# The identity multiplied into an unread PSUM bank while TensorE waits, and a shorter setup, in a four-layer graph kernel

## The reference, cut to what matters

```python
A_norm = A + jnp.eye(n)
deg = jnp.sum(A_norm, axis=0) + jnp.sum(A_norm, axis=1) - jnp.diagonal(A_norm)
dinv = jax.lax.rsqrt(deg)
A_hat = A_norm * dinv[:, None] * dinv[None, :]
agg = jnp.einsum('nm,bmd->bnd', A_hat, features)
h = jax.nn.relu(_batchnorm(agg @ W1.T + b1, g1, be1))   # 256 features, over all 32*256 rows
out = _batchnorm(h @ W2.T + b2, g2, be2)                # 128 features, over all rows
x = _layernorm(x + out)
# layer 1: edge attention over 256 edges; layer 2: three adjacency convolutions; layer 3: dense attention
```

## Time and profile before

| | |
|---|---|
| median of 3 runs | 604.58 us |
| the profiled execution, its time | 603.32 us |
| its span | 601.4 us |
| mean granted clock | 0.95 of full |
| TensorE matmul busy | 539.0 us (90%) |
| VectorE busy | 429.6 us (71%) |
| ScalarE busy | 368.4 us (61%) |
| GpSimd busy | 218.3 us (36%) |

### The profile page before, as it was taken

How to read it: one execution, slowest core, us unless ns; L and a number is a source line. 1 busy time by engine, 2 the same in 40 slices (tenths; PEclk the granted TensorE clock), 3 DMA queues, 4 the chain that set the end, 5 groups by cost and what they waited for, 6 DMA issues and landing times.

```text
span 601.4 us, 11286 instructions
## 1 busy us (share of the span) xinstructions
PE 539.0 (90%) x3508; PEld 474.7 (79%) x3508; DVE 429.6 (71%) x1446; ACT 368.4 (61%) x733; POOL 218.3 (36%) x253
## 2 busy tenths in 40 slices
PE   2999799489999879999999999999999999999461
PEld 2888544368787779998998999999999999889361
DVE  5588668678886166358878688787687685756895
ACT  1567692657755415536587686785785776775460
POOL 6750340366575250503516216226126026021231
PEclk9999899789999769999999999999999999999787
DMA  6232100221200000000000100100100100001002
GB/s 188 76 99 70 37 0 0 70 71 36 70 0 1 1 1 1 1 1 1 1 1 2 36 0 1 35 0 0 35 0 0 36 0 10 25 1 37 1 2 70
DMA packets 28382, 15.25 MB, mean 25 GB/s; under 512 B 2320, under 2 KB 28048, under 8 KB 28352
## 3 DMA queue, kind: packets, MB, share of 16 engines
q1 hardware_dynamic: 27792, 13.65, 7.9%
q0 software_dynamic: 560, 1.25, 0.6%
HBM read 10.69 MB, written 4.19 MB: 25 GB/s over the span
## 4 chain that ended last, share of the span: by engine, by line
PE 78%; DVE 13%; ACT 4%; issue 2%; POOL 2%; DMA 1%; DVEq 0%; SPq 0%; ACTq 0%; POOLq 0%
PE psum L237 14%; PE psum L239 14%; PE psum L238 14%; PE psum L1507 9%; PE psum L1332 5%; PE psum L1374 4%; PE psum L1449 2%; PE psum L1459 2%; PE psum L1381 2%; PE psum L1385 2%; PE psum L1395 2%; PE psum L1535 2%; DVE ln_st L183 2%; PE psum L1553 2%; DVE soft L865 2%
## 5 line engine op out<-in xcount | busy, mean ns | idle before, releaser
L202 POOL TENSOR_TENSOR ln_r<-ln_v,mhalf 128x8 f32<-128x8 f32 x32 | 53.3, 1665 | 233.1 <-DVE ln_v L196 233.1
L1507 PE MATMUL psum<-l2w_s,h 128*128 128x128 f32 x512 | 59.7, 275 | 0.0
L1507 PEld LDWEIGHTS psum<-l2w_s,h 128*128 128x128 f32 x512 | 59.0, 192 | 0.7
L237 PE MATMUL psum<-qt_hi,l2w_s_hi 128*128 128x512 f32 x128 | 52.7, 412 | 0.0
L239 PE MATMUL psum<-qt_hi,l2w_s_lo 128*128 128x512 f32 x128 | 50.5, 395 | 0.0
L238 PE MATMUL psum<-qt_lo,l2w_s_hi 128*128 128x512 f32 x128 | 50.4, 394 | 0.0
L231 ACT ACTIVATE keep_x<-keep_x,ln_b,ln_r (+1 forms) x112 | 46.0, 486 | 2.7 <-POOL ln_b L205 2.7
L1175 ACT ACTIVATE h<-psum 128x512 f32<-128x512 f32 x64 | 37.3, 593 | 15.1 <-PE psum L239 15.1
L183 DVE BATCH_NORM_STATS2 ln_st<-keep_x 128x6 f32<-128x128 f32 (+1 forms) x192 | 39.3, 277 | 2.8 <-ACT keep_x L1102 1.7
L237 PE MATMUL psum<-wgt_hi,h_hi 128*128 128x256 f32 x128 | 37.4, 292 | 0.9 <-DVE h_lo L842 0.9
L865 DVE SCALAR_TENSOR_TENSOR soft<-keep_x,wa 128x128 f32<-128x128 f32 x128 | 38.0, 362 | 0.0
(11 more groups left out here) (225 smaller groups left out, 1766.0 us busy)
## 6 DMA issues: line engine op xcount, KB each, us to landing
xin<-in_x SPq DMA_DIRECT2D x64, 128.0 KB, 2.2
out_x<-ob SPq DMA_DIRECT2D x32, 128.0 KB, 1.8
l2w_raw<-in_l2w POOLq DMA_DIRECT2D x1, 512.0 KB, 6.5
adjs<-in_adj SPq DMA_DIRECT2D x1, 256.0 KB, 2.8
adjs<-in_adj_t SPq DMA_DIRECT2D x1, 256.0 KB, 2.9
l2w_s<-in_l2w POOLq DMA_DIRECT2D x1, 256.0 KB, 6.2
w_raw<-in_w_t SPq DMA_DIRECT2D x1, 128.0 KB, 3.2
w2t<-in_w_t SPq DMA_DIRECT2D x1, 128.0 KB, 3.0
```

Source lines behind the costliest of these rows:

```text
L202: pool.tensor_tensor(ln.r[:].rearrange("p s k -> p (s k)"), ln.v[:].rearrange("p s k -> p (s k)"), mhalf[:], ALU.pow).then_inc(ln.root, 1)
L237: pe.matmul(o, lhs[0], rhs[0], start=start, stop=False)
L1507: i = pe.matmul(bank(s)[:, 0, k * D:(k + 1) * D], h2[:, s, g, j * N + t * P:j * N + (t + 1) * P], l2w3_s[:, g, :], start=(g == 0), stop=(g ...
```

## The change

The kernel after differs in these parts.

- `spin(n, bank)` is new: n float32 matmuls of `ident` with `iota_row` (256 columns) into a bank that nobody reads before it is written anew. It stands at five places on TensorE: 4 at the very start, 4 behind the turned roots, 6 behind pass1's edge work, 3 behind pass2's adjacency columns, 6 ahead of the first gather.
- Degrees: the sums along rows come from the accumulating output of two `scalar_tensor_tensor` a tile on VectorE, so that the degree is a 128 x 2 tile. Its root and reciprocal are taken at that size, and TensorE turns them into PSUM bank 0 by two transposes. ScalarE copies the transposed adjacency into `at1`.
- The split of the first weights on VectorE stands behind x0_low(0).
- `coefficients`: `shift = bias - mean` stands ahead of the wait for the root. In the second norm (`turn == 2`) the root and its reciprocal are one power on GpSimd, and the last pair's copy to `oraw` stands inside `coefficients`.
- pass2's statistics read PSUM and stand ahead of the copy; TensorE waits for relu by halves.
- The activation table is loaded behind relu, ahead of the second norm.

```diff
...
@@ -473,6 +473,9 @@
             link(pool.tensor_scalar(same[:], diff[:], 0.0, None, ALU.is_equal))
             pool.tensor_scalar(reset[:], same[:], 1.0, BIG, ALU.subtract, ALU.mult)
 
+            pool.wait_ge(bn_eps, 1)
+            pool.tensor_tensor(bco[:, 1, 2:3], bagg[:, 2:3, 1], mhalf[:, 0:1], ALU.pow).then_inc(bn_root, 1)
+
             pool.wait_ge(adj_dst_out, 1)
             pool.tensor_tensor(prod[:], adj_dst[:], ssrc[:], ALU.mult).then_inc(picked, 1)
 
@@ -594,36 +597,28 @@
 
             dve.wait_ge(pz, 4)
             dve.wait_ge(s_adj, 32)
-            dve.tensor_tensor(degm[:], adj_sb, adjt_sb, ALU.add)
             for t in range(T):
                 blk = slice(t * P, (t + 1) * P)
-                i = dve.tensor_tensor(prod[:, t, blk], adj_sb[:, t, blk], ident[:], ALU.mult)
+                dve.scalar_tensor_tensor(out=degm[:, t, :], in0=adj_sb[:, t, :], scalar=1.0, in1=adjt_sb[:, t, :],
+                                         op0=ALU.mult, op1=ALU.add, accum_out=degc[:, 0, t:t + 1])
+                i = dve.scalar_tensor_tensor(out=prod[:, t, blk], in0=adj_sb[:, t, blk], scalar=1.0, in1=ident[:],
+                                             op0=ALU.mult, op1=ALU.mult, accum_out=degc[:, 1, t:t + 1])
             link(i)
-            for t in range(T):
-                blk = slice(t * P, (t + 1) * P)
-                i = dve.tensor_tensor(degm[:, t, blk], degm[:, t, blk], prod[:, t, blk], ALU.subtract)
-            link(i)
-            for t in range(T):
-                blk = slice(t * P, (t + 1) * P)
-                i = dve.tensor_tensor(degm[:, t, blk], degm[:, t, blk], ident[:], ALU.add)
-            i.then_inc(deg_ready, 1)
-
-            link(dve.tensor_copy(at1[:], adjt_sb))
+            dve.tensor_tensor(degc[:, 2, :], degc[:, 0, :], degc[:, 1, :], ALU.subtract).then_inc(deg_ready, 1)
+
+            dve.wait_ge(at_ready, 1)
             for t in range(T):
                 blk = slice(t * P, (t + 1) * P)
                 i = dve.tensor_tensor(at1[:, t, blk], at1[:, t, blk], ident[:], ALU.add)
             link(i)
 
-            dve.wait_ge(s_small, 16 * SMALL)
-            link(dve.tensor_copy(w1t[0][:], w1_raw[:]))
-            dve.tensor_tensor(w1t[1][:], w1_raw[:], w1t[0][:], ALU.subtract)
-
             dve.wait_ge(deg_root, 1)
-            dve.reciprocal(dinv_bc[:], root_bc[:])
-            link(dve.reciprocal(dinv[:], root[:]))
+            dve.reciprocal(dinv[:], root[:]).then_inc(dinv_ready, 1)
+
+            dve.wait_ge(dinv_spread, 1)
             for t in range(T):
                 i = dve.scalar_tensor_tensor(out=at1[:, t, :], in0=at1[:, t, :], scalar=dinv[:, t:t + 1],
-                                             in1=dinv_bc[:], op0=ALU.mult, op1=ALU.mult)
+                                             in1=bank(0)[:, 0, 0:N], op0=ALU.mult, op1=ALU.mult)
             link(i)
             link(dve.tensor_copy(a_hat[0][:], at1[:]))
             dve.tensor_tensor(a_hat[1][:], at1[:], a_hat[0][:], ALU.subtract).then_inc(a_hat_ready, 1)
@@ -647,6 +642,10 @@
                     i.then_inc(h_stat, 1)
 
             x0_low(0)
+
+            dve.wait_ge(s_small, 16 * SMALL)
+            link(dve.tensor_copy(w1t[0][:], w1_raw[:]))
+            dve.tensor_tensor(w1t[1][:], w1_raw[:], w1t[0][:], ALU.subtract)
             agg_low(0)
 
             dve.wait_ge(keys_compared, 1)
@@ -677,11 +676,16 @@
                 i.then_inc(bn_var, 1)
                 dve.wait_ge(bn_var, turn)
 
+                if turn == 2:
+                    dve.tensor_scalar(bagg[:, ks, 1], bagg[:, ks, 1], BN_EPS, None, ALU.add).then_inc(bn_eps, 1)
                 bn_link(dve.tensor_tensor(mean, bagg[:, ks, 0], bias, ALU.add))
+                if turn == 2:
+                    dve.tensor_copy(oraw[:, Q - 1, :], bank(1)[:, 0, :]).then_inc(o_out, 1)
+                bn_link(dve.tensor_tensor(shift, bias, mean, ALU.subtract))
 
                 dve.wait_ge(bn_root, turn)
-                bn_link(dve.reciprocal(rstd, rstd))
-                dve.tensor_tensor(shift, bias, mean, ALU.subtract)
+                if turn == 1:
+                    bn_link(dve.reciprocal(rstd, rstd))
                 bn_link(dve.tensor_tensor(scale, rstd, gamma, ALU.mult))
                 bn_link(dve.tensor_tensor(shift, shift, scale, ALU.mult))
                 return dve.tensor_tensor(shift, shift, beta, ALU.add)
@@ -690,13 +694,23 @@
                          bnp[:, 0:2], bnp[:, 2:4], bnp[:, 4:6], 1).then_inc(bn1_ready, 1)
 
 
-            with dve.Fori(0, IT) as p:
-                for s in range(2):
-                    q = 2 * p + s
-                    dve.wait_ge(o_done, q + 1)
-                    dve.tensor_copy(oraw[:, q, :], bank(s)[:, 0, :]).then_inc(o_out, 1)
-                    wait_apart(dve, dc, o_out, q + 1)
-                    dve.bn_stats(bst2[:, q, :], oraw[:, q, :]).then_inc(o_stat, 1)
+            def o_stats(p, s):
+
+                q = 2 * p + s
+                dve.wait_ge(o_done, q + 1)
+                dve.bn_stats(bst2[:, q, :], bank(s)[:, 0, :]).then_inc(o_stat, 1)
+
+            def o_copy(p, s):
+                q = 2 * p + s
+                dve.tensor_copy(oraw[:, q, :], bank(s)[:, 0, :]).then_inc(o_out, 1)
+
+            with dve.Fori(0, IT - 1) as p:
+                for s in range(2):
+                    o_stats(p, s)
+                    o_copy(p, s)
+            o_stats(IT - 1, 0)
+            o_copy(IT - 1, 0)
+            o_stats(IT - 1, 1)
             dve.wait_ge(o_stat, Q)
             coefficients(slice(2, 3), [bst2[:].rearrange("p q c -> p (q c)")],
                          bnp[:, 6:7], bnp[:, 7:8], bnp[:, 8:9], 2).then_inc(bn2_ready, 1)
@@ -1037,9 +1051,11 @@
                     act.activation(hraw[:, :, q, :], bank(2 + 2 * s, 2), ACT.Copy).then_inc(h_out, 1)
 
 
-            act.wait_ge(deg_done, 1)
-            act.activation(root_bc[:], bank(0)[:, 0, 0:N], ACT.Sqrt)
-            act.activation(root[:], bank(1)[:, 0, 0:T], ACT.Sqrt).then_inc(deg_root, 1)
+            act.wait_ge(s_adj, 32)
+            act.activation(at1[:], adjt_sb, ACT.Copy).then_inc(at_ready, 1)
+            act.wait_ge(deg_ready, 1)
+            act.wait_ge(pz, 9)
+            act.activation(root[:], degc[:, 2, :], ACT.Sqrt, bias=ones[:, 0:1]).then_inc(deg_root, 1)
 
             x0_high(0)
             with act.Fori(0, IT - 1) as p:
@@ -1064,12 +1080,13 @@
             act.wait_ge(bn1_ready, 1)
             with act.Fori(0, Q) as q:
                 for k in range(H0 // P):
-                    i = act.activation(hraw[:, k, q, :], hraw[:, k, q, :], ACT.Relu, bias=bco[:, 3, k:k + 1], scale=bco[:, 2, k:k + 1])
-                i.then_inc(relu_ready, 1)
+                    act.activation(hraw[:, k, q, :], hraw[:, k, q, :], ACT.Relu, bias=bco[:, 3, k:k + 1],
+                                   scale=bco[:, 2, k:k + 1]).then_inc(relu_ready, 1)
+
+            act.preload_act_table_set("natural_log_exp_and_others")
 
             act.wait_ge(adj_dst_done, 1)
             act.activation(adj_dst[:], bank(6)[:, 0, :].rearrange("p (t e) -> p t e", t=T), ACT.Copy).then_inc(adj_dst_out, 1)
-            bn_sqrt(slice(2, 3), 2)
             act.wait_ge(bn2_ready, 1)
 
             def bn_out(p, first):
@@ -1102,7 +1119,6 @@
                     i = act.activation(y, y, ACT.Identity, bias=ln0.b[:, 1, k:k + 1], scale=ln0.r[:, 1, k:k + 1])
                 i.then_inc(ln0_done[1], 2)
 
-            act.preload_act_table_set("natural_log_exp_and_others")
             for p in range(3):
                 bn_out(p, p == 0)
 
@@ -1269,14 +1285,19 @@
         @block.tensor
         def _(pe):
 
-            pe.wait_ge(deg_ready, 1)
+            pe.wait_ge(pz, 9)
+
+            def spin(n, psum_bank):
+
+                for _ in range(n):
+                    pe.matmul(bank(psum_bank)[:, 0, 0:N], ident[:], iota_row[:], start=True, stop=True)
+
+            spin(4, 7)
+            pe.wait_ge(dinv_ready, 1)
             for t in range(T):
-                pe.matmul(bank(0)[:, 0, 0:N], ones[:], degm[:, t, :], start=(t == 0), stop=(t == T - 1))
-            for m in range(T):
-                for t in range(T):
-                    i = pe.matmul(bank(1)[:, 0, m:m + 1], degm[:, t, m * P:(m + 1) * P], ones[:, 0:1],
-                                  start=(t == 0), stop=(t == T - 1))
-            i.then_inc(deg_done, 1)
+                i = pe.transpose(bank(0)[:, 0, t * P:(t + 1) * P], dinv[:, t:t + 1].broadcast_to([P, P]), ident[:])
+            i.then_inc(dinv_spread, 1)
+            spin(4, 7)
 
             pe.wait_ge(a_hat_ready, 1)
 
@@ -1319,16 +1340,17 @@
                     i = pe.matmul(bank(7)[:, 0, m:m + 1], perm[:, t, m * P:(m + 1) * P], ecol_f[:, 0, t:t + 1],
                                   start=(t == 0), stop=(t == ET - 1))
             i.then_inc(edges_sorted, 1)
+            spin(6, 0)
 
 
             def pass2(p, first):
                 for s in range(2):
                     q = 2 * p + s
```

(4 more changed lines are left out.)

8 lines of the change are left out of this document (4 added, 4 removed).

## The result

The kernel after takes 596.95 us in the median of 6 runs (594.06 to 598.62), the kernel before 604.68 in 6 runs (604.0 to 605.24). The ratio is 0.9864, with a 95% interval from 0.9836 to 0.9891.

The account below looks back on a forecast made before the run. TensorE, with 78% of the chain, was taken as the bound. Gains of 0.65 + 2.3 + 1.3 + 0.2 = 4.45 us took the profiled 603.32 to 598.9, as a median 600.1 us; range 597.3 to 602.7.

Parts of the forecast that it names:

- Part A: Setup and pass1: 2.75 us gained at iteration 1, less 2.1 for a clock fall, 0.65 us; bounds -0.2 and 2.75.
- GpSimd ends the keys at 17.34 + 1.84 = 19.18, for its edges land no earlier: Setup: the wait for sorted keys lets TensorE start iteration 1 at about 20.6, not 23.34, whatever the setup saves.
- The first rival: Pass1: the clock holds through iteration 0's wait, 2.75 us gained there, 6.55 in all, 598.0 us; chance 0.20.
- The fourth: Setup: keys later than 19.2, as x is fetched again beside the edges' DMAs; 1.5 us later is 601.6; chance 0.08.
- Part B: First norm and pass2: 3.2 us from full clock and earlier start, less 0.9 of bank stall, 2.3; bounds 1.4 and 3.2.
- Rival 2: Norms: spins don't hold the clock, pass2's low stretch stays, 2.2 us gained, 602.4 us; chance 0.15.
- Rival 3: Pass2: the bank stall is the bound if PSUM statistics are slow; gain gone at s = 1.26; chance 0.03.
- Part C: Second norm: table load leaves the path, coefficients ready at about 107.3 as before; 1.3 us gained, bounds 0.3 and 2.25.
- Part D: First gather and behind: clock at the first transposes even, 0.2 us gained; spins ahead of the gather don't move the end.
- what that chain has gained is kept to the end: Behind the first gather: the layer norm chain's gain stays, with 0.5 us either way for later idle times' clock.

Follow-up runs that it names:

- the keys at 20.16: Kernel after with three more comparisons on GpSimd ahead of the keys, so that these come late: 600.55 us, ratio 0.9934.
- four banks: Kernel after with pass2 turning over four PSUM banks instead of two: 596.73 us, ratio 0.9844.
- three more spins: Kernel after with three more groups of spins, ahead of the second gather, the first attend1 and the third: 591.34 us, ratio 0.9773.
- the low part ahead of the keys: Kernel after with x0_low(1) ahead of the wait for the sorted keys on VectorE: 594.99 us, ratio 0.9839.

## Why the prediction was wrong

**Part A failed, at the step "GpSimd ends the keys at 17.34 + 1.84 = 19.18, for its edges land no earlier".** I took a DMA's landing as given, since the change touches no DMA. But it takes a VectorE copy away from the time when the edges' DMAs run. The copy alone, moved to ScalarE, brings the edges 2.2 us sooner, and put back on VectorE it brings them back to 13.98. With GpSimd's own work 0.8 us shorter as well, the keys end 2.91 us sooner. Of the 5.57 us at pass1's end, 2.75 are the gain that Part A had worked out for keys at 19.18, and 2.9 are the keys. Everything that it put behind the step hung on it: the idle time was 1.09 us and not 2.3 to 3.3, so the 2.1 us taken off for the clock never came. 2.9 and 2.1 make up, to 0.1 us, the 4.9 us between 0.65 and 5.57. That the wait for the keys is the cap was right (with the keys at 20.16 the edge work comes 4.90 us later), that an idle time of 4.68 us brings the low clock was right, and its price was half of what I said. Pass1's start was forecast at 10.5 and came at 10.38. The first rival had the gain at 2.75 and no fall; it too kept the edges' landing. The fourth had considered that the landing might move, but only later.

**Part B** was right in its mechanism and mis-sized in the stall. Pass2 began 0.73 us sooner by itself (0.86 forecast), with the clock at 1.00; the idle time was 0.84 (0.9 forecast). The stall was 1.8 us, the upper bound, where I took 0.9: TensorE's weight load follows the end of the copy by 0.27 us (77.60 to 77.87), and I had allowed 0.12 for it. B gained 0.73 + 0.55 = 1.3 us and not 2.3, and four banks gave the 1.7 us back at pass2's end. Rival 2, that spins don't hold the clock, is out: with them the clock is 1.00 in 60 to 70, without them 0.50 in 66 to 68. Rival 3 is out as well, since statistics from PSUM take 0.70 us, as from SBUF.

**Part C** was right: 1.5 us (6.85 to 8.37) where 1.3 were forecast. The load left the path, the power took 0.58 (0.4 forecast), and the product behind was held until `prod` was through. The Trainium skill (GPSIMD Engine Reference, Key points), which has GpSimd contend with VectorE instructions of two SBUF inputs, agrees with 1.11 us beside `prod` and 0.16 without it. The Trainium skill (ScalarE: Activation LUTs, What ACT_TABLE_LOAD costs), with its drain of 1.38 us on top, would have made C 2.7; the trace has 1.5.

**Part D** was right as far as it went: full clock at the first transposes behind 1.91 us (called even, and with three more spins further on the clock did fall there), a gather pushed by low spins (4.35 us) without harm to the second gather, which stood 9.05 us sooner. But then "what that chain has gained is kept to the end", 0.5 us either way, was too sure. The kernel after loses 1.5 us by `attend1`, all of it in the second gather (5.35 us for 16 records that take 3.8 at full clock), and 3.2 in all in the profiled execution. In others it loses less: the mean clock was 0.957 in the profiled one of 597.42 us and 0.965 in the one of 594.06. Three spins further on hold 5.6 us.

**The sum.** Up to the second gather the gain is 4.45 + 4.9 (A) - 1.0 (B) + 0.2 (C) + 0.5 (D) = 9.05 us, as the table has it. The profiled executions differ by 5.9 us, so 3.15 of it were given back; the medians differ by 7.7, so there it would be about 1.35 (an estimate, with the same 9.05 up to the gather). The forecast had nothing given back, which hid part of its error in A. The range was too narrow at its lower end, since I had let the edges' landing move in one direction only. With the keys held back to 20.16 the time is 600.55, inside the range.

## What to carry to other kernels

Before an input's landing is taken as a fixed cap, look at what the change adds to or takes from the other engines while that DMA runs: here one VectorE copy of 0.42 us, moved to ScalarE, went with edges that were there 2.2 us sooner. Look as well at what stands behind a wait in the written order: the split of the first weights waited for DMAs until 8.80 us, and with it ahead of the reciprocal pass1 started 2.82 us later (13.29 against 10.47). The reciprocal of 1.75 us was worth 1.1 at iteration 1 (19.94 against 18.86). A gain ahead of a chain of waits is kept only if TensorE's later idle times don't bring the low clock: list the idle times behind the change, from about 2 us on, and price each at both clocks, since the same idle time went with either clock here. Where such an idle time can't go, matmuls into an unread bank mostly hold the clock, but they have to stand in all of these places and to end before the awaited data come.

## What the runs showed of the hardware

- With a VectorE copy of 128 x 512 from SBUF to SBUF, 0.42 us, moved to ScalarE, the DMAs of the next microseconds ran faster: 221, 213 and 339 GB/s in 8 to 11 us instead of 95, 67 and 167, and the edges were there 2.2 us sooner. Whether the copy or the second table load beside its move does it is not shown.
- Two-input GpSimd work of 1.3 us holds a one-column VectorE product until its own end: 1.11 us instead of 0.16.
- The length of an idle time alone didn't tell the clock. Behind 3.20, 3.55, 4.25 and 4.68 us it was low at the first record. Behind 3.17 us ahead of the second gather it fell 0.1 us into the gather (kernel after), and with the low part ahead of the keys not at all. Behind 2.45 us ahead of `attend1` it was full in the kernel after and low with four banks (0.54 in 191 to 195). Behind 0.84 to 1.91 us it was full at the first record, but fell soon behind such idle times too: near 107.9 in the kernel after, and near 101.6 with three more spins.
- Spins mostly hold a clock (the three ahead of the first transposes did in the kernel after, and didn't in the one with three more groups), and run at the low one if it has fallen already: 6 of them took 2.76 us at full and 4.35 us with the clock low until 111.4.
